# Attention scores and maxima: pairs of the same kind in place of a score item beside a maximum item

## What is computed

```
x = x + attn_a(layernorm(x))
x = x + ffn(layernorm(x), Wg, Wu, Wd)
x = x + attn_b(layernorm(x), w_in, w_out)
x = x + ffn(layernorm(x), Wg, Wu, Wd)

# attn_b
scores = einsum('bhqd,bhkd->bhqk', q, k) * scale + alibi_bias   # -inf where key > query
attn = softmax(scores);  ctx = einsum('bhqk,bhkd->bhqd', attn, v);  out = ctx @ w_out.T
```

## Time and profile before

| what | value |
|---|---|
| median of 3 runs | 1679.25 us (1678.73 to 1680.9) |
| the profiled execution, its own time | 1676.88 us |
| its span | 1675.1 us |
| mean granted TensorE clock | 0.996 |
| busy: PE, DVE, ACT, POOL | 1636.6, 1272.8, 1063.6, 248.1 us |
| first item of units 0, 1, 7, 15 | at 723.1, 755.7, 905.4, 1105.2 us |
| a unit with maxima, without projection | 24.1 us |

### The profile page before, as it was taken

The page is one execution under the profiler, slowest core; times in us unless marked ns, Lnnn a source line. Parts: engine busy times, 40 slices in busy tenths (PEclk is TensorE's granted clock), DMA queues, the critical chain, the costliest instruction groups (busy, mean ns, idle before and its releaser), DMA issues.

```text
span 1675.1 us, 28454 instructions
## 1 busy us (share of the span) xinstructions
PE 1636.6 (98%) x10387; PEld 1170.9 (70%) x10387; DVE 1272.8 (76%) x2541; ACT 1063.6 (63%) x1976; POOL 248.1 (15%) x469
## 2 busy tenths in 40 slices
PE   6999999999999999999999999999999999999998
PEld 4668787887778887754444544438888888888887
DVE  6789677776877777789999999946666666666665
ACT  6555765675566565578888888885555555555554
POOL 6522001200210113421211221220000000000000
PEclk9999999999999999999999999999999999999999
DMA  7000011002000023223212111100000000000000
GB/s 226 1 0 1 1 30 34 1 1 55 12 1 1 25 90 113 89 83 97 63 28 65 46 47 52 28 3 1 7 1 7 1 7 7 1 7 7 1 7 7
DMA packets 63446, 52.46 MB, mean 31 GB/s; under 512 B 7999, under 2 KB 58574, under 8 KB 63310
## 3 DMA queue, kind: packets, MB, share of 16 engines
q1 hardware_dynamic: 63136, 50.57, 10.4%
q10 hardware_dynamic: 174, 0.07, 0.0%
HBM read 32.40 MB, written 18.22 MB: 30 GB/s over the span
## 4 chain that ended last, share of the span: by engine, by line
PE 89%; DVE 6%; ACT 3%; issue 1%; POOL 0%; DMA 0%; DVEq 0%; SPq 0%; POOLq 0%
PE ps L1380 7%; PE ps L1417 7%; PE ps L1418 7%; PE ps L1419 7%; PE ps L1251 7%; PE ps L1252 6%; PE ps L1253 6%; PE ps L1196 6%; PE ps L933 4%; PE ps L1441 4%; PE ps L1442 4%; PE ps L1443 3%; PE ps L1267 3%; PE ps L1269 3%; PE ps L1268 3%; PE ps L1179 3%
## 5 line engine op out<-in xcount | busy, mean ns | idle before, releaser
L2392 DVE SCALAR_TENSOR_TENSOR hid<-sg,ps 128x512 f32<-128x512 f32 x256 | 175.7, 686 | 183.7 <-PE ps L1419 182.9
L1848 ACT ACTIVATE sg<-ps 128x512 f32<-128x512 f32 x256 | 153.3, 599 | 236.2 <-PE ps L1419 234.6
L1762 ACT ACTIVATE sg<-ps 128x512 f32<-128x512 f32 x256 | 153.4, 599 | 200.3 <-PE ps L1253 195.1
L2254 DVE TENSOR_TENSOR hid<-sg,ps 128x512 f32<-128x512 f32 x256 | 174.8, 683 | 136.9 <-PE ps L1253 95.8
L2244 DVE TENSOR_REDUCE negp<-ps 128x1 f32<-128x512 f32 (+2 forms) x450 | 243.3, 611 | 8.2 <-PE ps L1179 6.8
L1757 ACT ACTIVATE pr<-ps 128x512 f32<-128x512 f32 x384 | 206.4, 601 | 48.1 <-PE ps L1171 30.5
L1251 PE MATMUL ps<-xn_hi,w_hi 128*128 128x512 f32 x510 | 209.1, 410 | 0.0
L1417 PE MATMUL ps<-xn_hi,w_hi 128*128 128x512 f32 x512 | 202.5, 395 | 0.0
L1418 PE MATMUL ps<-xn_lo,w_hi 128*128 128x512 f32 x512 | 200.2, 391 | 0.0
L1252 PE MATMUL ps<-xn_lo,w_hi 128*128 128x512 f32 x510 | 199.8, 392 | 0.0
L1253 PE MATMUL ps<-xn_hi,w_lo 128*128 128x512 f32 x510 | 199.7, 392 | 0.0
(11 more groups left out here) (293 smaller groups left out, 3068.7 us busy)
## 6 DMA issues: line engine op xcount, KB each, us to landing
qs<-qd SPq DMA_DIRECT2D x60, 96.0 KB
ks<-kd SPq DMA_DIRECT2D x60, 96.0 KB
kd<-qkp SPq DMA_DIRECT2D x14, 256.0 KB, 2.9
qd<-qkp SPq DMA_DIRECT2D x7, 384.0 KB, 2.6
w_raw<-in_Wg SPq DMA_DIRECT2D x4, 512.0 KB, 7.3
w_raw<-in_Wu SPq DMA_DIRECT2D x4, 512.0 KB, 7.4
w_raw<-in_Wd SPq DMA_DIRECT2D x4, 512.0 KB, 8.9
work<-hd SPq DMA_DIRECT2D x8, 256.0 KB, 5.0
```

## The change

`score_and_max` is no longer called in `unit`. At an even place k, PE issues the score items k and k+1 side by side, in the two halves; at the odd place after it, the maximum items k-1 and k side by side. What followed place k before follows it still, so the values, transposes and the projection at an even place now stand between the two score items and the two maximum items. Masks are issued in turns for the two halves; the semaphores "scores" and "job" are signalled with each item's last instruction. Banks, the values that are waited for, and the programs of the other engines are the same. The call at the end of the feed-forward layer stays.

```diff
--- before.py
+++ after.py
@@ -1241,6 +1241,39 @@
                             jm = job_mask(k // 2, je, j_dst, j_parts[i], table) or jm
                 if with_job:
                     jm.then_inc(T["job"], 1)
+
+            def score_pair(n, items):
+
+                done = {}
+                for i in range(len(score_parts(items[0]))):
+                    for k in items:
+                        nth = n * NG_S + k
+                        if i == 0 and nth >= len(S_BANKS):
+                            pe.wait_ge(T["exp"], nth + 1 - len(S_BANKS))
+                        done[k] = score_main(n, k % 2, score_bank(n, k), score_parts(k)[i])
+                    for k in items:
+                        done[k] = score_mask(k % 2, score_bank(n, k), score_parts(k)[i]) or done[k]
+                for k in items:
+                    done[k].then_inc(T["scores"], 1)
+
+            def max_pair(n, items):
+
+                done = {}
+                for i in range(len(job_parts(items[0] // 2))):
+                    for k in items:
+                        if i == 0 and k in (0, JOBS_KC1):
+                            nxt = (n + 1) % SLOTS
+                            pe.wait_ge(T[f"loaded{nxt}{1 if k == 0 else 0}"], ((n + 1) // SLOTS + 1) * LOADS)
+                        ago = n * NG_S + k - len(J_BANKS)
+                        if i == 0:
+                            pe.wait_ge(T["reduced"],
+                                       reduced_to(ago // NG_S + 1, ago % NG_S) if ago >= 0 else EARLY_REDUCES)
+                        done[k] = job_main(k // 2, n + 1, 1 - k % 2, job_bank(n, k), job_parts(k // 2)[i])
+                    for table in range(2):
+                        for k in items:
+                            done[k] = job_mask(k // 2, 1 - k % 2, job_bank(n, k), job_parts(k // 2)[i], table) or done[k]
+                for k in items:
+                    done[k].then_inc(T["job"], 1)
 
             def ffn(f):
 
@@ -1488,8 +1521,10 @@
                         for c in range(2):
                             if k == FIRST_OF_C[c]:
                                 pe.wait_ge(T[f"m_loaded{c}"], n * 32 + 32)
-                        if (n, k) != (0, 0):
-                            score_and_max(n, k)
+                        if k % 2 == 0:
+                            score_pair(n, (1,) if (n, k) == (0, 0) else (k, k + 1))
+                        elif n < LAST_UNIT:
+                            max_pair(n, (1,) if (n, k) == (0, 1) else (k - 1, k))
                         if k == OWN_MAXIMA:
                             if n:
                                 pe.wait_ge(T["ctx"], n * 2 - 1)
```

## The result

The changed kernel takes **1742.78 us** in the median of 4 runs (1741.58 to 1744.1), beside 1678.99 us for the kernel before in the same measurement. The ratio is 1.038, 95% interval 1.0363 to 1.0399: slower by 3.8%. The forecast was 1738, the range 1704 to 1754.

What follows compares the result with a forecast made beforehand. DVE paces the attention, with PE close behind. 14 units at 4.0 us (56), unit 0 2 and unit 15 1 make 59 us on 1676.88, so 1735.9; with 2.4 for the median, 1738 us, range 1704 to 1754.

Steps and rivals of the forecast that it cites:

- What bounds it: Attention stage: DVE sets the pace with PE close behind; three banks leave 0.07 us of idle time after the values of 15.
- Packing worth nothing: PE in attention: pairing was costed at nothing, 0.57 us for two masked items before against 0.59 after.
- The ladder: DVE stalls per unit: 1.00 us (place 18), 0.80 (10), 0.85 (26), 0.55 (2), odd places 1.1; 4.3 in all; chance 0.74.
- The wait that it rests on: Score item k+1 waits for exponential k-2 ahead of the values; without it place 18 stalls 0.33 us, not 1.00.
- the order: Even places: values stand between score pair and maximum pair, ahead of maximum item k; alone 0.33 us stall at 18.
- Odd places: After values at odd places the next maximum stands behind a score pair: 0.23 us each at 16, 24; together 1.1.
- The later signal of a masked pair: Place 30, masked maximum pair: both items signal at the end of the pair, costing 0.13 us.
- The discount: Attention unit total taken as 4.0 us, not 4.3, since a stall lets the exponentials catch up before the next.
- The projection units: Three attention units whose projection copy and matmuls now precede maximum items 18 and 26; 5.0 us a unit as upper bound.
- Only the order bites: Rival: in attention the exponential is ready in time, because DVE's stalls give ACT time; 1704 to 1715 us; chance 0.14.
- Worse than the ladder: Rival: PE's pauses lower its granted clock, or the stalls chain up; over 1754 us; chance 0.04.

Runs made afterwards that it cites:

- the second experiment: Changed kernel with the second score item behind the values again, maxima still paired behind them (S V S J J): 1721.90 us, ratio 1.0259.
- the first: Changed kernel with scores in pairs but maxima issued singly, one ahead of the values again (S S J V J): 1720.80 us, ratio 1.0255.
- the fourth experiment: Changed kernel with the two maxima of a pair issued one after the other, each with its masks and signal: 1742.38 us, ratio 1.0381.
- the first five experiments: Edits of the changed kernel: maxima singly 1720.80 us; second score behind values 1721.90; even values one place later 1710.87; paired maxima in turn 1742.38; maxima first 1754.38.

## Why the prediction was right, and where not

The profiled execution grew by 1743.87 - 1676.88 = 67.0 us. The units' first items give where: 0.3 before the attention, 1.2 in unit 0, 61.8 in units 1 to 14 (757.3 to 1168.6 against 755.7 to 1105.2), 3.5 in unit 15, 0.1 behind it. The prediction had 0, 2, 56, 1 and 0.

- **What bounds it** was read rightly. DVE paced the attention, the cover of three banks was used up at each V (0.07 us left), and everything that PE does later came out as a DVE stall. DVE's waits in 300 us rose to 51 us; "about 50" was said.
- **Packing worth nothing** holds. Pairs apart from values, three in a unit, change the time by a ratio of 1.0007, and taking the maxima of a pair in turn changes nothing. The Trainium skill, TensorE: Matmul & The Clock Gate, section Packing small matmuls, has matmuls in strict program order, which would have made the pair at 30-31 cheaper than its two single items; no run here shows that gain (a unit of 24.2 us with pairs apart, 24.1 without).
- **The ladder held.** It counts how much later a reduce starts, while the brackets in the rows count how long DVE is idle, and that is 0.08 us less at each stall: a reduce lasts 0.68 us, but the next one starts 0.60 after it where nothing holds it up (the prediction's 0.61 has two late starts in it). By starts, R(16) to R(18) take 948.33 - 946.15 = 2.18 us, against 1.21 before: 0.97, where 1.00 was forecast. In the same way place 10 gives 0.83 for 0.80, place 26 0.81 for 0.85, place 2 0.45 for 0.55. The wait that it rests on is there: S(19) starts 0.05 us after E(16) ends (0.06 forecast), and 1.10 us after S(16) (1.12). Of the idle time at these four places the second experiment puts 1.51 us on the order and 1.37 on the wait; the first, which undoes the order, leaves 1.06 for the wait.
- **Odd places: the sum right, the places not.** By starts, 0.24 at 16 and 0.29 at 24 (0.23 each forecast), 0.06 at 30 for 0.36, 0.56 at 32 for 0.3, and 0.07 at 34, where nothing was forecast: 1.2 for 1.1. That 30 and 32 make up for each other is luck. The later signal of a masked pair, which I had put in at 30, is nil by the fourth experiment.
- **The discount was the term mis-sized.** The ladder gave 4.3 us a unit, its places measure 4.3 by starts, and the unit grew by 4.4. I had taken 4.0, arguing that a stall lets the E's catch up. There was nothing to catch up: in the change as before, ACT had been idle for 0.63 us when E(16) started, so E(16) follows S(16) at once in both. (DVE's idle time, 4.3 us a unit against 0.3, happens to have grown by just 4.0; the rest shows as busy time, 24.1 us in place of 23.7, as back-to-back reduces overlap less.) Over 14 units the growth is 61.8 us where 56 was forecast, 5.8 too little; with 2.5 more in unit 15, 0.8 less in unit 0 and 0.4 outside it makes the 8 us between 59 and 67. In medians the miss is 5 us (63.8 against 58.7), as the profiled execution of before lies 2.1 us under its median and that of the change 1.1 above.
- **The projection units** were to cost about the same as the others, or 5.0 as upper bound; they cost 4.7 (27.4 to 32.1), most of it before R(18) and R(26).
- **"Only the order bites"** is refuted by the second experiment: without the wait the time is 1722, not 1743. (It is also above the 1704 to 1715 that the rival gave: the order alone was priced too low.)
- **"Worse than the ladder"** named a falling clock and gave it no weight by unit 15 of before, and in unit 15 it came: 2.65 of the 3.5 us there. The other 0.9 are the order, forecast as 1. It is small, but there what I read in the profile of before did not carry over.

What stays open: why the clock falls in unit 15 of some executions and not of others, why unit 0 costs 1.2 us and not 2, and why place 30 costs so much less and 32 more than forecast.

## What to carry to other kernels

Where an engine with a short queue of buffers paces a stage, count the time that the feeding engine is away between two refills, and not its total work: the S pair of 0.23 us left DVE idle for 0.26 to 0.28 us behind most of the V at odd places, while pairs away from V cost nothing. An instruction with a wait should stand behind long work that doesn't need it, not ahead of it: the same score item ahead of the values instead of behind them cost 1.4 us a unit at the four even places. Before two kinds of work are sorted into pairs for better packing, look in the trace whether they run side by side already.

## What the runs showed of the hardware that was not expected

TensorE's granted clock fell from full speed (2.4 GHz) to 0.5 (1.2 GHz) for 6.8 us in unit 15 of the changed kernel, though no unit with maxima, with DVE stalls of up to 2.1 us, showed it after unit 0. What the engine did before doesn't tell why. The first row is that slow stretch. The others are the first 4.5 us of unit 15 in the kernel before, where no fall follows, the same in the kernel with the transpose at 31, and the fall that follows there. The instructions of unit 15 are the same in these two kernels.

```profile
1172.80:1179.60 6.80, 6.54 (x26) 1.10 (x26) 1.70 (x11) 3.95 (x8) 0.00 (x0) 0.50 0.02 4
```

```profile
1105.20:1109.70 4.50, 3.58 (x25) 1.18 (x21) 0.63 (x3) 4.04 (x11) 1.19 (x5) 1.00 0.00 0
```

```profile
1105.20:1109.70 4.50, 3.58 (x25) 1.21 (x21) 0.59 (x3) 4.07 (x10) 1.20 (x5) 1.00 0.00 0
1109.70:1113.10 3.40, 3.40 (x16) 0.48 (x15) 1.70 (x11) 2.11 (x5) 0.00 (x0) 0.50 0.03 7
```

PE is busy for 3.58 of 4.5 us in both, and the clock falls in one of them. A fall of 3.4 to 10.2 us came in unit 15 of the traced execution of nine kernels: the change, the first five experiments, the two called "single items" with values at odd places and with the transpose at 31, and the one with single items in the last unit only. None came in the kernel before, with the values at 31 and with pairs apart. This holds for the one execution of each that was traced, and others of the same kernel may differ: the four of the change had a mean granted clock of 0.994, 0.995, 0.996 and 0.996 and took 1743.87, 1744.1, 1741.68 and 1741.58 us. The last two are about 2.3 us shorter, near the 2.65 us that a fall of 6.8 us costs; whether theirs was shorter or missing was not traced.

Matmuls overtake each other between the halves of the rows, as the kernel before had shown (J(1) at 905.59, S(1), ahead of it in the program, at 905.72). With the maxima of a pair issued in turn, the unit kept its length to 0.02 us, so there the order between the halves didn't matter.
